# Two token chunks stay on chip between the projection and the MLP of a transformer block

## The reference

```python
ada = silu(c) @ W_ada + b_ada          # shift, scale, gate for attention and for the MLP
h = modulate(layernorm(x), shift_msa, scale_msa)
x = x + gate_msa * attention(h)        # 16 heads of 36, softmax, projection 576 -> 576
h = modulate(layernorm(x), shift_mlp, scale_mlp)
mlp = gelu(h @ W_fc1 + b_fc1) @ W_fc2 + b_fc2      # 576 -> 2304 -> 576
x = x + gate_mlp * mlp
```

## Time and profile before

| | us |
|---|---|
| median of 3 runs | 3611.79 (3610.05 to 3613.69) |
| the profiled execution, its own time | 3609.45 |
| its span in the profile | 3607.4 |
| PE busy | 3518.7 (98%) |
| PEld, DVE, ACT, POOL busy | 2257.5, 1883.7, 1559.3, 361.6 |
| mean granted TensorE clock | 0.990 |

### The profile page before, as it was taken

The page is one execution under the profiler, slowest core; times in us unless marked ns, Lnnn a source line. Parts: engine busy times, 40 slices in busy tenths (PEclk is TensorE's granted clock), DMA queues, the critical chain, the costliest instruction groups (busy, mean ns, idle before and its releaser), DMA issues. The chain is left out here.

```text
span 3607.4 us, 46334 instructions
## 1 busy us (share of the span) xinstructions
PE 3518.7 (98%) x16996; PEld 2257.5 (63%) x16996; DVE 1883.7 (52%) x3411; ACT 1559.3 (43%) x2908; POOL 361.6 (10%) x284
## 2 busy tenths in 40 slices
PE   7999999999999999999999999998969999999999
PEld 5888844444444444444444444436859899898988
DVE  5446566666666666666666666624542323333232
ACT  3223256565665655656556556564540101111010
POOL 1000010111100000000000000024501010000000
PEclk9999999999999999999999999999989999999999
DMA  5453421212111121212111111115662231422221
GB/s 191 163 170 139 141 79 29 58 42 54 40 36 45 29 52 29 54 29 51 32 46 35 33 47 29 32 34 197 225 220 97 70 103 60 145 83 92 73 86 50
DMA packets 147040, 290.25 MB, mean 80 GB/s; under 512 B 18354, under 2 KB 44210, under 8 KB 139904
## 3 DMA queue, kind: packets, MB, share of 16 engines
q1 hardware_dynamic: 145604, 287.28, 25.7%
q10 hardware_dynamic: 1216, 0.00, 0.0%
HBM read 181.81 MB, written 104.34 MB: 79 GB/s over the span
## 5 line engine op out<-in xcount | busy, mean ns | idle before, releaser
L1068 DVE TENSOR_REDUCE q_mx<-b_sp 128x1 f32<-128x512 f32 x1976 | 1203.2, 679 | 614.2 <-PE b_sp L1009 614.2
L1117 ACT ACTIVATE b_pt<-b_st 128x512 f32<-128x512 f32 x2048 | 1031.0, 626 | 783.3 <-PE b_st L1027 783.2
L1038 PE MATMUL b_op<-b_pt,b_vs 128*37 128x512 f32 x4096 | 931.0, 597 | 0.0
L1038 PEld LDWEIGHTS b_op<-b_pt,b_vs 128*37 128x37 f32 x4096 | 223.9, 114 | 538.7 <-issue 459.1
L1749 ACT ACTIVATE d_af<-d_pf,d_b 128x512 f32<-128x512 f32 x144 | 99.1, 688 | 747.7 <-PE d_pf L1671 746.9
L1688 PE MATMUL d_pm<-d_vl,d_ah 128*128 128x288 f32 x1152 | 340.8, 296 | 0.0
L1689 PE MATMUL d_pm<-d_vh,d_al 128*128 128x288 f32 x1152 | 340.5, 296 | 0.0
L1687 PE MATMUL d_pm<-d_vh,d_ah 128*128 128x288 f32 x1152 | 340.5, 296 | 0.0
L1182 POOL TENSOR_TENSOR w_oc<-b_oa,b_ob 37x512 f32<-37x512 f32 x128 | 161.4, 1261 | 1722.7 <-ACT b_ob L1129 1711.5
L1009 PE MATMUL b_sp<-q_hh,q_lo 108*128 108x512 f32 x696 | 295.6, 425 | 4.5 <-PEq L831 4.5
L1027 PE MATMUL b_st<-q_lo,q_hh 110*128 110x512 f32 x704 | 275.2, 413 | 1.8 <-ACT b_pt L1117 1.8
(11 more groups left out here) (265 smaller groups left out, 4610.6 us busy)
## 6 DMA issues: line engine op xcount, KB each, us to landing
d_hh<-hth SPq DMA_DIRECT2D x16, 1280.0 KB, 6.5
qkh<-a_th SPq DMA_DIRECT2D x72, 256.0 KB, 2.0
qkl<-a_tl SPq DMA_DIRECT2D x72, 256.0 KB, 2.2
d_yi<-y SPq DMA_DIRECT2D x64, 288.0 KB, 3.0
d_hl<-htl SPq DMA_DIRECT2D x16, 1024.0 KB, 8.8
vd<-a_vx SPq DMA_DIRECT2D x8, 1184.0 KB, 6.4
b_vs<-vd SPq DMA_DIRECT2D x32, 296.0 KB, 2.8
a_x<-in_x SPq DMA_DIRECT2D x8, 1152.0 KB, 6.2
```

The lines of the kernel that those rows point to most:

```text
L1038: ins = e.matmul(op[blk % 2][64 * a:64 * a + VW, :], vs[h % 2][:, 2 * j + a, :], pt[g % NP][:, a * 512:a * 512 + 512], start=j == 0, stop= ...
L1068: e.tensor_reduce(mx[:, k // 4, k % 4:k % 4 + 1], sp[slot % 3][:, :], AX.X, ALU.max).then_inc(s_mx, 1)
L1117: e.activation(pt[g % NP][:, a * 512:a * 512 + 512], st[x % 3][:, :], ACT.Exp, scale=SCALE).then_inc(s_p, 1)
```

## The change

Chunk 0's and chunk 7's normed tokens are written into tiles that live on through the MLP: `N.hh[0]`, `N.hl[0]` are the attention's old `hh0`, `lo0`, and `N.hh[1]`, `N.hl[1]` are `ah0`, `al0`. The MLP takes the chunks in the order 0, 7, 1, ..., 6 and reloads them from HBM from the third on. fc1 tiles 0 to 2 of chunk 0 move from the MLP into the end of `work()`. Chunk 7's last `stats` moves ahead of chunk 6's last `back`. Two of chunk 7's four `xn` quarters move from ACT to DVE. Chunk 7's store moves into the MLP. Weight pieces 5 to 8 are loaded in the projection, into the token tile `oi`; the bias `b1` is loaded at its second chunk; pieces 9 and 10 go ahead of the four broadcasts.

```diff
+class Ahead:
+    def __init__(self, S, hh, hl, b1):
+        self.hh, self.hl, self.b1 = hh, hl, b1
+        self.oi = S.sb("oi", [128, KT, CH])
+        stg = self.oi[:, :, :].rearrange("p k t -> p (k t)")
+        self.stg = [stg[:, i * C:(i + 1) * C] for i in range(4)]
+        self.pf = [S.ps(f"pf{i}", [128, 512]) for i in range(4)]
...
@@ phase_proj
+        if c == SPARE:
+            places[7] = stats(c)[3:] + places[7]
         if c:
             places[7] += turn2(c - 1)[5:]
...
-        for p in stats(NCH - 1)[3:] + norm(NCH - 1) + turn2(NCH - 1):
+        back = turn2(SPARE)
+        for p in norm(SPARE) + [("fc1", 0, 0)] + back[0:4] + [("fc1", 0, 1)] + back[4:5] + [("fc1", 0, 2)]:
             yield p
...
+                if c == 1:
+                    e.dma_start(N.b1[:, :], b_fc1.rearrange("(f p) -> p f", p=128),
+                                allow_slow_non_contiguous=True).then_inc(N.s_b1, 16)
...
+            elif kind == "project" and c == SPARE and n < 4:
+                e.wait_ge(s_u, KT * NCH)
+                i = (5 + n) % 4
+                e.dma_start(N.stg[i][:, 0:FF // 6], W_fc1[n * 128:n * 128 + 128, FF // 6:FF // 3]).then_inc(N.s_w[i], 16)
...
-        e.wait_ge(s_hs, 32)
+        e.wait_ge(N.s_b1, 16)
...
+            elif kind == "fc1":
...
+                e.wait_ge(s_x1, 8 * NCH - 3 + n)
+                pairs = passes(first.wh, first.wl, first.wm, first.wr, N.hh[0], N.hl[0], slice(n * 128, n * 128 + 128),
+                               slice(0, CH))
...
+            elif kind == "xn" and c == SPARE and n > 1:
+                e.wait_ge(s_nb, c + 1)
+                e.wait_ge(s_tb, KT * c)
+                for a, z, d in ((0, C, 0), (512, C, C)):
+                    ins = e.tensor_scalar(xn[:, n, d:d + z - a], x1[c % 2][:, n, a:z], rs[i][:, n:n + 1], nb[i][:, n:n + 1],
+                                          ALU.mult, ALU.add)
@@ phase_mlp
+    ORDER = [0, NCH - 1] + list(range(1, NCH - 1))
...
-        return range(DONE + 2 * m, DONE + 2 * m + 2 if m < NT - 1 else W1[1]) if m < NT else range(0)
+        k = DONE + 2 * m + 2
+        return range(k if m else DONE, min(k + 2, W1[1])) if m < NT else range(0)
...
-        load(0)
-        e.dma_start(b1[:, :], b_fc1.rearrange("(f p) -> p f", p=128), allow_slow_non_contiguous=True).then_inc(s_b1, 16)
-        for k in range(DONE, DONE + 4):
+        for k in range(DONE + 4, DONE + 6):
             load_w(k)
...
+        rows = slice((NCH - 1) * CH, NCH * CH)
+        e.dma_start(hth[:, :, rows].rearrange("k p t -> p k t"), hh[1][:, :, :].bitcast(F)).then_inc(N.s_hs, 16)
+        e.dma_start(htl[:, :, rows].rearrange("k p t -> p k t"), hl[1][:, :, :].bitcast(F)).then_inc(N.s_hs, 16)
...
-            for f in range(NT):
+            for f in range(3 if n == 0 else 0, NT):
...
+                    if m == 3 and p % 3 == 0:
+                        e.wait_ge(s_whi, p // 3 + 1)
+                        e.wait_ge(s_wlo, p // 3 + 1)
```

More of the change, by code:

```diff
@@ L262, in program @@
                 first = FirstThird(E, w0)
+                ah0, al0 = E.sb("ah0", [128, KT, CH], R), qs0[:, :].rearrange("p (k t) -> p k t", k=4)
                 with ExitStack() as last:
-                    W = Prefetch(Scope(nc, last, "w", top), w0, qs0)
+                    W = Prefetch(Scope(nc, last, "w", top), w0, ah0, al0)
                     with ExitStack() as ctx:
@@ L267, in program @@
                                         W_proj, b_proj, xf, qkh, qkl, vd, ot, sm)
+                    N = Ahead(Scope(nc, late, "n", top, "right"), [hh0, ah0], [lo0, al0],
+                              mx[:, :, :].rearrange("p q k -> p (q k)")[:, 0:FF // 128])
                     with ExitStack() as ctx:
[L269 to L272, removed]
+                        phase_proj(nc, Scope(nc, ctx, "c", top), W, first, N, ident, ks0, adaT, eps, gd, xf, ot, sm,
+                                   W_fc1, b_fc1, hth, htl, y1)
+                with ExitStack() as ctx:
+                    phase_mlp(nc, Scope(nc, ctx, "d", top), first, N, gd, hth, htl, y1, y2, of, W_fc1, b_fc1, W_fc2, b_fc2)
 def phase_qkv(nc, A, ident, adaT, eps, bq, sc, qs0, ks0, qs1, ks1, hh0, lo0, mx, nm, mh, ml, gd, xf, cond, W_ada,
@@ L1225, in phase_proj @@
     pt = [A.ps(f"pt{i}", [128, 512]) for i in range(4)]
-    pm = [A.ps(f"pm{i}", [128, 512]) for i in range(4)]
+    pm = N.pf
     s_a, s_x, s_xg, s_ta, s_u, s_ah, s_al = W.s_a, W.s_x, W.s_xg, W.s_ta, W.s_u, W.s_ah, W.s_al
@@ L1294, in h_out @@
     def h_out(c):
[L1295 removed]
+        if c in (0, SPARE):
+            return N.hh[c % 2], N.hl[c % 2]
+        return hh, hl
     def h_free(e, c):
@@ L1372, in tensor @@
                 ins.then_inc(s_tb, 1)
+            elif kind == "fc1":
+                if n == 0:
+                    e.wait_ge(first.hi, KT)
+                    e.wait_ge(first.lo, KT)
+                    e.wait_ge(s_hh, KT)
+                    e.wait_ge(s_hl, KT)
+                e.wait_ge(s_x1, 8 * NCH - 3 + n)
+                pairs = passes(first.wh, first.wl, first.wm, first.wr, N.hh[0], N.hl[0], slice(n * 128, n * 128 + 128),
+                               slice(0, CH))
+                for p, (w, a) in enumerate(pairs):
+                    ins = e.matmul(N.pf[n][:, :], w, a, start=p == 0, stop=p == 13)
+                ins.then_inc(N.s_f1, 1)
             elif kind == "project":
@@ L1466, in scalar @@
                 e.activation(sd[i][:, :], mv[i][:, :, 1], ACT.Sqrt, bias=eps[:, 0:1]).then_inc(s_sd, 1)
-            elif kind == "xn":
+            elif kind == "xn" and (c < SPARE or n < 2):
                 e.wait_ge(s_nb, c + 1)
@@ L1519, in phase_proj, with phase_mlp @@
         block.gpsimd(gpsimd)
-def phase_mlp(nc, A, first, gd, hth, htl, y1, y2, of, W_fc1, b_fc1, W_fc2, b_fc2):
+def phase_mlp(nc, A, first, N, gd, hth, htl, y1, y2, of, W_fc1, b_fc1, W_fc2, b_fc2):
     NT = FF // 2 // 128
```

70 lines of the change are left out of this document (35 added, 35 removed).

## The result

The changed kernel takes 3580.05 us (median of 4 runs, 3576.74 to 3584.57); the kernel before, timed beside it, 3610.92 (3601.90 to 3613.69). The ratio is 0.9921, with a 95% interval from 0.9906 to 0.9936: between 23 and 34 us faster. The forecast was 3584, in a range of 3578 to 3592. The profiled execution took 3576.74 us, with a span of 3574.8.

What follows compares the result with a forecast made beforehand. PE was taken to be full, busy 98% of the span, so gains come only from holes in its time. Terms 10.5 + 21.1 - 1.7 - 2.3 = 27.6 us, against the median 3611.79, gave 3584; range 3578 to 3592.

Steps and rivals of the forecast that it cites:

- Up to the blocks, 10.5 us: End of projection: the MLP begins at 2648.7 instead of 2659.17, 10.5 us earlier.
- Blocks to tile 3, 21.1 us: From the MLP's beginning to tile 3's first matmul: 1.35 us instead of 22.5, saving 21.1.
- Inside tile 3, 1.7 us lost: PE uses pieces 5 to 8, then waits for piece 9; tile 3 ends at 2655.0, 1.7 us lost.
- Ahead of tile 6, 2.3 us lost: Tile 6 needs piece 14, loaded behind the broadcasts and finished by DVE near 2664: 2.3 us lost.
- now with less ahead of them, they land near 2658: Ahead of tile 6: the four broadcasts, issued at 2651.5, land near 2658; pieces 11 to 14 follow until 2660.
- The clock stays full: Across the seam PE was supposed to keep the full clock, the new gap ahead of the transposes being 1.8 us.
- The rival of the clock: At the seam, bursts between gaps keep PE's clock low: 13 us at half, 6.5 us more, 3591; 10%.
- From fc2 on, nothing: From the first fc2 tile to the end: no PE wait and no further gain or loss.
- The signs of being wrong: Clock at 0.50 between 2640 and 2665, landings of pieces 9 to 14 over 5 us, or PE stopping in first fc2 tile.
- second rival: Weight pieces 9 to 23 through four staging tiles set fc2's start: 8 us more, 3592, or 24 more, 3608; 10%.
- Table load: Before GELU 0 on ACT: 1.28 us; by the 2.66 rule tile 3 ends 1.4 later, the sum stays.
- The range's lower end, 3578: Lower end of the forecast range: no loss within tiles 3 to 8 and a release 1 us earlier.

Runs made afterwards that it cites:

- the norm's order: Kernel before with only the last tile's statistics ahead of the remaining back turns and two of four `xn` on DVE: 3607.78 us, ratio 0.9982 to 1.0001.
- broadcasts late: Changed kernel with the four broadcasts of gt and gb (MLP second half's gate and bias) issued behind weight pieces 11 to 14 instead of ahead: 3571.97 us.
- 448 bytes: Changed kernel with the four broadcasts behind the weight pieces and 448 unused bytes allocated ahead of the MLP's weights: 3571.77 us.
- tiles 3 and 4 in turn: Changed kernel with broadcasts behind the weight pieces, 448 unused bytes ahead of the MLP's buffers, and first chunk's tiles 3 and 4 alternating on PE: 3569.78 us.
- tokens placed first: Kernel before with the MLP's four token buffers allocated ahead of the weights instead of behind them, no instruction touched: 3598.36 us.

## Why the prediction was right, and where it was not

- **Up to the blocks, 10.5 us.** Measured 25.41 - 14.74 = 10.7. The mechanism is shown: 3.3 by the norm's order (run with it alone), 7.8 by the store that nobody waits for (8.1 against 0.3), less 0.5 because PE and not DVE closes the block. Two small misses cancelled: PE was through 14.5 us behind the last x1 tile (2628.23 to 2642.69) where the prediction has 13.8, and the change of blocks took 0.3 us, not 1.0.
- **Blocks to tile 3, 21.1 us.** Before 22.49, after 1.35 (2642.97 to 2644.32). Right to the hundredth as a stretch. But as the worth of its parts it is no sum: tiles 0 to 2 beside the norm are worth 7.6 us with the broadcasts late and nothing with them ahead, and the early pieces 2.8 and 0.3. The prediction treated the losses further on as small corrections; they were what tied the parts together.
- **Inside tile 3, 1.7 us lost.** Measured 1.8, and gone when tile 4 covers it.
- **Ahead of tile 6, 2.3 us lost: too small.** Measured 4.9. The step that failed is "now with less ahead of them, they land near 2658": in its count 6.5 us for the broadcasts. They took 9.7, from 2645.99 to POOL's product at 2655.65, no less than the 8.4 of the earlier trace rows, and piece 11, issued behind them, 8.1. From the first broadcast to the end of piece 14 on DVE it was 15.2 us (to 2661.14) instead of 12.5, which is the whole of the error. The slowed DVE was in the count and came out.
- **The clock stays full: wrong.** It fell in the wait ahead of tile 6 and cost 2.9 us (half of 5.76). The rival of the clock was ruled down because no gap reached 3 us; this one reached 4.9 because of the step before. By the Trainium skill, "TensorE: Matmul & The Clock Gate", HAM oscillation, bursts that are shorter than the waits between them each start at the low clock. Here there was one long wait, and the clock was back at full 5.8 us behind it.
- **From fc2 on, nothing: wrong by 5.0 us.** PE does the same matmuls in 57.76 and 57.90 us a chunk instead of 58.23, about 6.2 us in all, less 1.2 for the new wait at 3124.40, which the prediction didn't have either. The runs that move buffers, in the kernel before and in the changed one, show that place alone moves the pace; that it is the whole of these 6.2 us is inferred, since in the changed kernel the order of the chunks is another too.
- **The signs of being wrong.** The prediction names three. Two came: the clock was 0.50 between 2660 and 2667, and a piece took over 5 us to land (8.1). They mark its second rival, the stream of pieces, which it gave 10%: that mechanism was at work, for one piece and not for four rounds. By its own signs the prediction was wrong here, though the time is right.
- **Table load.** 1.28 us, and the GELU 0.02 behind it. The drain that the Trainium skill adds to the load ("ScalarE: Activation LUTs", What ACT_TABLE_LOAD costs) isn't in the row.

The seam: 10.7 + 21.1 - 1.8 - 4.9 - 2.9 - 0.2 (the tiles' own pace) = 22.0 us, where the prediction had 27.6. With the 5.0 behind it, 27.0. So the total was right by luck: an error of 5.6 was met by a gain of 5.0 that nobody had forecast. (The range's lower end, 3578, is 1 us under what its own terms give, 3584.2 - 4.0 - 1.0 = 3579.2; nothing hangs on it.)

The other 5.5 us of the profiled executions are not the change's. In the ten executions of the changed kernel and its variants, which but for the four early DMAs are one program up to the last x1 tile, that tile starts between 2627.94 and 2636.65; in the three of the kernel before and its variants between 2632.17 and 2635.44. The medians differ by 30.9, and the interval, 23 to 34, holds the 27.0.

Windows over the stall of the projection: before, changed, broadcasts late.

```profile
2505.00:2545.00 40.00, 28.25 (x157) 25.11 (x156) 16.40 (x37) 16.39 (x29) 13.94 (x12) 0.74 0.59 196
```

```profile
2505.00:2545.00 40.00, 28.29 (x187) 25.65 (x185) 19.29 (x41) 18.20 (x31) 17.58 (x13) 0.83 0.56 193
```

```profile
2505.00:2545.00 40.00, 28.28 (x158) 25.16 (x157) 16.99 (x36) 16.50 (x28) 14.23 (x11) 0.74 0.57 192
```

PE is busy as long in all three, but at a mean clock of 0.74, 0.83 and 0.74: the changed kernel and the one with the broadcasts late are the same program up to there, and in one of them the clock came back later. This makes 3.6 us against the kernel before (40 times 0.09). The other 1.8 us the changed kernel had gained by the end of attention (SP's last issue there is at 2446.67, at 2448.51 in the earlier trace rows), with a mean clock of 0.99 against 0.97 from 2380 to 2450.

## What to carry to other kernels

Parts of a change that shorten the same stretch are not a sum: price each with the others in and out, and look which stream of transfers ends last once they are all in. Constants that are needed late should not be issued ahead of the pieces that the next tile waits for; that single move was worth about 8 us, more than the early load and about as much as the tiles made beside the norm. The token load ahead of the second half's pieces is another such place: it cost the profiled execution of the changed kernel 1.2 us, and no run here moved it. And a wait on TensorE can cost twice, itself and the half clock behind it. At this seam every wait of 3.1 to 5.2 us did, in all runs, and of the shorter ones, 1.6 to 2.0 us, only two: 1.8 with the 448 bytes, 2.0 with tiles 3 and 4 in turn.

## What the runs showed of the hardware that was not expected

The pace of matmuls with 4-byte operands hangs on where weights and tokens lie in on-chip memory. Addresses in bytes of a partition, from the programs' allocations; ns from one matmul's start to the next's, means over the steady MLP:

| fc1, moving 512 columns | tokens mod 512 | weights mod 512 | ns |
|---|---|---|---|
| before, `d_wh` | 128 | 32 | 233.4 |
| before, `e_wh` | 128 | 480, 224 | 234.3 |
| tokens placed first, `d_wh` | 32 | 32 | 226.7 |
| tokens placed first, `e_wh` | 32 | 480, 224 | 229.0 |
| broadcasts late, even chunks, `d_wh` | 288 | 352 | 233.3 |
| 448 bytes, even chunks, `d_wh` | 288 | 288 | 226.7 |

(`e_wh` is 576 columns wide, so its strips lie in turn at two addresses modulo 512.) Fc2, moving 288 columns, took 133.3 ns with the two operands at 32 and 0 modulo 64 (before, and with the tokens placed first), and 132.6 with both at 32 (changed, and with 448 bytes). For fc1 the agreement modulo 512 was forecast once and came out; for fc2 it is only read from four kernels. Why it is so, and why the odd chunks of the kernel with 448 bytes lost 0.18 us, stays open.
